# Late query and key normalisation moved within its attention pair, and the order of the PSUM bank pairs for the first transposes swapped

## What is computed

```
x = x + layernorm(attention(layernorm(x)))
x = x + layernorm(ffn(layernorm(x)))

attention(x):  q = rms_norm(x @ wq.T, q_norm_w)      # 32 heads of 64
               k = rms_norm(x @ wk.T, k_norm_w)      # 8 heads of 64, each used by 4 query heads
               v = x @ wv.T
               scores = q k^T / 8 + slope_h * (s - t),  allowed only for 0 <= t - s <= 256
               return (softmax(scores) v) @ wo.T
ffn(x):        ((silu(x @ gate_w.T * gate_s) * (x @ up_w.T * up_s)) @ down_w.T) * down_s
```

## Time and profile before

| | us |
|---|---|
| median of 3 runs (lowest, highest) | 1207.07 (1206.99, 1207.17) |
| the profiled execution | 1205.83 |
| its span in the profile | 1204.1 |
| PE busy | 1163.0 (97%) |
| DVE busy | 896.2 (74%) |
| ACT busy | 745.7 (62%) |
| POOL busy | 304.9 (25%) |

### The profile page before, as it was taken

The page is one execution under the profiler, slowest core; times in us unless marked ns, Lnnn a source line. Parts: engine busy times, 40 slices in busy tenths (PEclk is TensorE's granted clock), DMA queues, the critical chain, the costliest instruction groups (busy, mean ns, idle before and its releaser), DMA issues.

```text
span 1204.1 us, 26656 instructions
## 1 busy us (share of the span) xinstructions
PE 1163.0 (97%) x9016; PEld 990.8 (82%) x9016; DVE 896.2 (74%) x2328; ACT 745.7 (62%) x1582; POOL 304.9 (25%) x353
## 2 busy tenths in 40 slices
PE   7999999999999999999999999999999999999997
PEld 5778888887778888888888898898888888888876
DVE  5587878687898888888888888888866575546464
ACT  4546555556999877777778788888862443222230
POOL 3000000001788733323333423233311100202022
PEclk9999999999999999999999999999999999999999
DMA  5316355347676756355645654557436440303020
GB/s 175 105 44 245 141 215 204 140 193 257 222 235 221 249 178 232 124 188 195 205 148 169 214 190 153 170 179 214 141 95 227 147 130 30 105 1 105 1 70 36
DMA packets 100898, 189.55 MB, mean 157 GB/s; under 512 B 9376, under 2 KB 39072, under 8 KB 100768
## 3 DMA queue, kind: packets, MB, share of 16 engines
q1 hardware_dynamic: 100768, 187.88, 46.1%
HBM read 116.22 MB, written 71.63 MB: 156 GB/s over the span
## 4 chain that ended last, share of the span: by engine, by line
PE 91%; DVE 4%; ACT 2%; issue 2%; DMA 0%; POOL 0%; SPq 0%; DVEq 0%; POOLq 0%; ACTq 0%
PE bank L1408 21%; PE bank L1541 19%; PE bank L1473 15%; PE bank L1346 12%; PE bank L1434 12%; PE bank L1452 3%; PE bank L1450 3%; PE bank L1451 3%; PE bank L1462 2%; DVE pT_lo L1168 1%; PE bank L1518 1%; PE bank L1373 0%; DVE pT_lo L1172 0%; ACT y_raw L937 0%; PE bank L1363 0%
## 5 line engine op out<-in xcount | busy, mean ns | idle before, releaser
L802 ACT ACTIVATE p_sb<-u_sb,low 128x384 f32<-128x384 f32 (+2 forms) x512 | 271.9, 535 | 63.2 <-DVE low L1054 54.7
L1054 DVE CUSTOM_DVE_ANT_0 u_sb<-bank,bias 128x384 f32<-128x384 f32 (+2 forms) x512 | 229.3, 452 | 45.0 <-PE bank L1346 23.5
L1346 PE MATMUL bank<-k_st,q_st 128*128 128x384 f32 (+2 forms) x1024 | 252.4, 329 | 0.5 <-DVE low L1054 0.4
L1434 PE MATMUL bank<-ident,p_sb 128*128 128x128 f32 x1152 | 217.8, 280 | 23.8 <-DVE pT_lo L1168 13.0
L1168 DVE TENSOR_TENSOR pT_lo<-bank,pT_hi 128x384 f16<-128x384 f32 (+2 forms) x392 | 178.3, 455 | 37.1 <-ACT pT_hi L913 29.7
L1434 PEld LDWEIGHTS bank<-ident,p_sb 128*128 128x128 f32 x1152 | 139.2, 140 | 57.4 <-issue 25.1
L913 ACT ACTIVATE pT_hi<-bank 128x384 f16<-128x384 f32 (+2 forms) x392 | 159.6, 407 | 39.4 <-PE bank L1434 36.1
L1346 PEld LDWEIGHTS bank<-k_st,q_st 128*128 128x128 f32 x1024 | 169.3, 192 | 17.2 <-DVE low L1054 0.9
L696 POOL TENSOR_TENSOR o_out<-o_raw,inv_sum 128x256 f32<-128x256 f32 x128 | 80.3, 628 | 308.1 <-DVE inv_sum L1180 308.1
L1541 PE MATMUL bank<-zT_hi,gu 128*128 128x512 f32 x352 | 139.3, 396 | 0.6 <-DVE hid L1297 0.6
L1541 PE MATMUL bank<-zT_lo,gu 128*128 128x512 f32 x352 | 138.3, 393 | 0.0
(11 more groups left out here) (134 smaller groups left out, 2317.5 us busy)
## 6 DMA issues: line engine op xcount, KB each, us to landing
q_st<-q_scr SPq DMA_DIRECT2D x32, 1024.0 KB, 8.0
q_scr<-qk SPq DMA_DIRECT2D x61, 512.0 KB, 2.7
k_st<-k_scr SPq DMA_DIRECT2D x64, 256.0 KB, 3.3
o_scr<-o_out SPq DMA_DIRECT2D x128, 128.0 KB, 3.7
o_in<-o_scr SPq DMA_DIRECT2D x16, 768.0 KB, 5.6
z_in<-z_scr SPq DMA_DIRECT2D x8, 1024.0 KB, 6.2
k_scr<-qk SPq DMA_DIRECT2D x12, 512.0 KB, 2.7
v_scr<-v_out SPq DMA_DIRECT2D x4, 1040.0 KB, 6.5
```

Of the source, the lines that this page charges most:

```text
L802: nc.scalar.activation(p_sb[:, u % RING, 0:w], u_sb[:, u % RING, 0:w], ACT.Exp, scale=-1.0, bias=low[:, u % RING:u % RING + 1]).then_inc(p ...
L1054: nc.vector.tensor_tensor_reduce(out=u_sb[:, u % RING, 0:w], in0=bank[u % 2][:, 0:w], in1=bias[2 * u // UNITS][:, u % REP, at:at + w], sca ...
L1346: mm = nc.tensor.matmul(bank[u % 2][:, 0:w], q_st[:, s, r, P * i:P * i + P], k_st[:, s, part, P * key:P * key + w], start=(part == 0), sto ...
L1434: mm = nc.tensor.transpose(bank[probability_bank(A)][:, P * j:P * j + P], p_sb[:, u % RING, P * j:P * j + P], ident[:])
```

## The change

Three places are edited.

1. `LATE_AT` for the count 1: the late norm of pairs 4 to 10 stands at unit 17 and no longer at unit 8.
2. `probability_bank`: the two bank pairs of the twins change places, so units 0 and 1 are transposed into banks 6 and 7, units 2 and 3 into banks 2 and 3. The wait for the value tiles goes with the banks, from units 0 and 1 to units 2 and 3.
3. `TWINS` falls from 120 to 118, so that the last twin lies in banks 6 and 7 and the first single in banks 2 and 3; units 22 and 23 of pair 3 become singles.

```
-TWINS = LAG * UNITS - 2 * TT
+TWINS = LAG * UNITS - 2 * TT - 2
...
-LATE_AT = {4: (2, 4, 18, 20), 3: (4, 18, 20), 1: (8,)}
+LATE_AT = {4: (2, 4, 18, 20), 3: (4, 18, 20), 1: (17,)}
...
-    return unit % 2 + (6 if unit < TWINS and unit // 2 % 2 else 2)
+    return unit % 2 + (6 if unit < TWINS and unit // 2 % 2 == 0 else 2)
...
-                if n == 0 and u < 2:
-                    pe.wait_ge(v_ready, TT * (B - 1) + 2 + u + 1)
+                if n == 0 and u in (2, 3):
+                    pe.wait_ge(v_ready, TT * (B - 1) + u + 1)
```

## The result

| | before | after |
|---|---|---|
| median (lowest to highest), us | 1207.03 (1206.67 to 1207.17) | 1193.56 (1192.59 to 1194.10) |
| profiled execution, its span | 1205.83, 1204.1 | 1192.59, 1190.7 |
| PE busy | 1163.0 | 1161.0 |

The ratio is 0.9888 with a 95% interval of 0.9871 to 0.9905. The change is faster by 13.5 us, and 1194.0 was forecast.

The account below looks back on a forecast made before the run. PE, busy 97%, waits for DVE and DVE for POOL at unit 8. Profiled 1205.83 - 14.1 (leaving unit 8) + 1.0 (unit 17), start and TWINS 0, gives 1192.7; as median 1207.07 - 13.1 = 1194.0 us, range 1191.9 to 1198.1.

Parts of the forecast that it names:

- The price of unit 8: Late norm leaving unit 8 saves 2.03 us a pair in pairs 5 to 10, 12.2 us; with pair 4, 14.1.
- The low bound of 11.5 us: Least gain from moving the late norm off unit 8: only PE's listed waits in pairs 4 to 10, 11.5 us.
- Pair 4: Not comparable as a whole, having no tile norm of its own; gain at unit 8 estimated at 1.9 us.
- Unit 17: Late norm's new place in pairs 4 to 10: costs 0.15 us a pair, 1.0 in all, bounds 0 to 4.6.
- The start: Attention's start: PE's 1.08 us wait for the last value tile becomes other idleness; gain 0, bounds +1 to -1.5 us.
- the rival of a start without the fall: At the attention's start PE's clock doesn't fall: 1.5 us less, 1192.5 us; chance 0.05.
- TWINS: One twin becomes two singles, 0.16 us on DVE and about as much on ACT, once: 0, bounds -0.3 and +0.3.
- The product as a whole in the chain of ORs: At unit 17 the whole product delays the ORs: 4.6 us in place of 1.0, 1197.6 us; chance 0.13.
- No change: Unit 8's wait stays because the split of the transposed output behind it is late: 1207.07 us; chance 0.04.
- slower: At unit 17 all three late-norm pieces lie on PE's path, 2.49 a pair against 2.03 gained: 1210.3 us; chance 0.04.
- The OR held until the division is over: Behind unit 17 the OR waits for all of POOL's division, 0.31 late: 1.9 us in all, 1194.9; chance 0.12.
- The price of a late OR: Read from pair 6: every microsecond by which a pair's first OR is late costs about 0.85 us.

Follow-up runs that it names:

- bias_after_8: Kernel before, late norm still at unit 8, but POOL's first bias of pairs 4 to 15 placed behind the pair's first group division: 1198.60 us, ratio 0.9931.
- banks_only: Changed kernel with the late norm back at unit 8, so only the banks and TWINS differ from before: 1206.92 us, ratio 1.0002.
- ahead2_old_banks: Changed kernel with banks and TWINS as before, and DVE's biases of units 2 and 3 ahead of the last value tile's read: 1193.34 us, ratio 0.9891.
- late16: Changed kernel with the late norm of pairs 4 to 10 at unit 16, one unit earlier: 1193.47 us, ratio 0.9888.
- bias_at_17: Changed kernel with POOL's second bias of pairs 4 to 10 one group division earlier, running while unit 17's product is due: 1200.64 us, ratio 0.9939.

## Why the prediction was right

- **The price of unit 8.** 2.03 us a pair was read from pairs that do the same with and without a late norm. That held: less the 0.11 that the late norm costs at its new place it is 1.92, and pairs 5 to 10 became shorter by (245.00 - 233.47)/6 = 1.92 each. Its reason held as well, and bias_after_8 splits the 2.03 in 1.08 for POOL's hold and 0.95 for the norm itself. The low bound of 11.5 us, the listed waits alone, took the list for the whole cost, which it isn't: a wait costs some 0.16 us more than its listed idle time.
- **Pair 4.** An estimate of 1.9 us less 0.15; measured 39.72 - 37.92 = 1.80.
- **Unit 17.** 0.15 us a pair was charged, 1.0 in all; measured is 38.84 - 38.73 = 0.11, 0.8 in all. The steps are in the rows: the product at the end of unit 17's bias, the split of unit 15 0.66 behind it, no new wait at PE's transposition, 0.11 us left of the idle 0.37, where about 0.1 was worked out, the division 0.25 later and the OR held by it for 0.16 us, where 0.11 was worked out.
- **The start.** 0 was taken, with PE's wait going over to the bias of unit 2; the wait is 1.67 us, within the 1.5 to 1.9 named, and banks_only is 1.0002 of before. The clock still falls; the rival of a start without the fall didn't come true here, but ahead2_old_banks, whose start is another, shows that it can happen there, and it was worth 1.0 to 1.1 us, less than the 1.5 put on it.
- **TWINS.** 0 was taken within 0.3 either way; it costs 0.14.
- **The rivals.** The product as a whole in the chain of ORs is refuted by pairs of 38.84. No change and slower are refuted by the waits, which are gone at unit 8 and didn't come at unit 17. The OR held until the division is over is half true: it is held, for 0.16 in place of 0.31 us. The Trainium skill's rule ("SBUF — State Buffer", "Who interferes with whom") agrees with this trace in which instructions exclude each other; its "for the whole instruction" holds up to some 0.2 us: in the kernel after, the OR ends 0.55 us after the profile's end of the division, where its own length is 0.69. Whether the hold really ends early, or the profile shows the division's end late, these runs don't tell.
- **The price of a late OR.** The 0.85 us per microsecond came from pair 6, whose first OR is 0.28 us late for a reason that the profile calls issue. That pair is a weak measure: with the same 0.28 us its surplus over the plain pairs is 0.24 us before, 0.17 after (39.01 against 38.84) and 0.36 in late16 (39.13 against 38.77, there with a new wait of PE of 0.24 us). Pair 5 was left in the plain price, though it too is longer than pair 7, by 0.15 us before and after; in both kernels it holds PE's wait for `y_raw`. By an estimate from these surpluses none of this moved the forecast by more than 1 us.

What stays unexplained is that issue time of pair 6; its cause wasn't looked for.

## What to carry to other kernels

Before an instruction is moved off the critical stretch, look at how long it takes there against its shortest elsewhere: a DVE instruction of 1.82 us, where the same one elsewhere takes 0.75, is waiting inside its own duration, and no list of waits names it. Then two numbers place it anew: what POOL does at that moment, and how long DVE is idle within the next steps. The kernel after has one such instruction left: in pair 2 a product of the same shape takes 1.12 us from 356.38, beside a cast of POOL that ends at 356.95. A wait lifted at a stage's start is worth nothing while the next instruction in the same queue waits for an engine that is late anyway; read that next start first.

## What the runs showed of the hardware

- A held instruction of DVE shows as a longer one, not as idleness: 1.82 and 1.73 against 0.75 us behind POOL's bias, 0.85 and 1.06 against 0.69 us behind a division. In all four cases it ends 0.54 or 0.55 us after POOL's instruction; a split with one input in PSUM isn't held (0.56 us beside the bias in bias_at_17).
- An idle stretch of PE costs more than its listed length: 1.58 us between two starts for 1.42 listed.
- The lower level of PE's clock, 1.2 GHz, came behind the idle stretches at the attention's start in 12 of the 13 profiles and was absent in one, ahead2_old_banks, whose start another kernel repeated with the fall. Of two executions with the same start it makes about 1 us: 29.38 against 30.37.
